# Reloading K of a half group in four transfers, one per batch, instead of one

## What is computed

```python
def attention(query, key, value):          # 8 x 128 x 512 each; key and value are both ctx
    q = (query @ Wq).reshape(nb, q_len, H, D).transpose(0, 2, 1, 3)      # H = 32, D = 128
    k = (key @ Wk).reshape(nb, q_len, KVH, D).transpose(0, 2, 1, 3)      # KVH = 8
    v = (value @ Wv).reshape(nb, q_len, KVH, D).transpose(0, 2, 1, 3)
    q = q * cos + _rotate_half(q) * sin
    k = k * cos + _rotate_half(k) * sin
    k, v = repeat(k, 4), repeat(v, 4)
    scores = where(mask == 0, -1e9, q @ k.T / sqrt(D))
    return (softmax(scores) @ v).reshape(nb, q_len, H * D) @ Wo
x = x + tanh(g_xattn) * attention(layernorm(x), ctx, ctx)
x = x + tanh(g_ffn) * (silu(x1) * x2 @ w3.T + b3)     # x1, x2 = split(layernorm(x) @ w12.T + b12)
```

## Time and profile before

| | us |
|---|---|
| median of three runs | 636.28 |
| lowest and highest | 635.9, 636.29 |
| the profiled execution, its own time | 636.77 |
| its span, first to last instruction | 634.9 |
| TensorE (PE) busy in it | 623.6 |
| POOL busy | 450.3 |
| VectorE (DVE) busy | 482.8 |
| ScalarE (ACT) busy | 319.2 |

### The profile page before, as it was taken

The page is one execution under the profiler, slowest core; times in us unless marked ns, Lnnn a source line. Parts: engine busy times, 40 slices in busy tenths (PEclk is TensorE's granted clock), DMA queues, the critical chain, the costliest instruction groups (busy, mean ns, idle before and its releaser), DMA issues.

```text
span 634.9 us, 10094 instructions
## 1 busy us (share of the span) xinstructions
PE 623.6 (98%) x2865; PEld 511.7 (81%) x2865; DVE 482.8 (76%) x1235; ACT 319.2 (50%) x893; POOL 450.3 (71%) x374
## 2 busy tenths in 40 slices
PE   8999999998999999999999999999999999999997
PEld 7888888876888877787888788888778788888886
DVE  3987675797878878788878788878885998976342
ACT  5435622554764646455455555554634657545310
POOL 6456866898889898888898898988886677601100
PEclk9999999999999999999999999999999999999999
DMA  9997995156587686776677676876645413000002
GB/s 300 324 324 227 295 321 166 70 188 211 178 266 230 201 249 207 240 244 213 196 244 241 211 245 221 261 234 213 216 139 176 131 50 90 0 2 1 0 34 99
DMA packets 133990, 118.38 MB, mean 186 GB/s; under 512 B 9776, under 2 KB 104496, under 8 KB 133936
## 3 DMA queue, kind: packets, MB, share of 16 engines
q1 hardware_dynamic: 132512, 116.69, 57.7%
q0 software_dynamic: 384, 1.05, 0.5%
q10 hardware_dynamic: 1040, 0.00, 0.1%
HBM read 72.89 MB, written 44.83 MB: 185 GB/s over the span
## 4 chain that ended last, share of the span: by engine, by line
PE 69%; DVE 9%; POOL 8%; DMA 7%; issue 4%; ACT 3%; DVEq 0%; POOLq 0%; ACTq 0%; SPq 0%
PE f_bank L889 9%; PE f_bank L891 9%; PE f_bank L890 9%; PE o_bank L889 7%; PE o_bank L891 7%; PE o_bank L890 7%; DMA p<-p_scratch 3%; DVE t_sin L2417 3%; PE pv_bank L889 3%; PE pv_bank L891 3%; PE pv_bank L890 3%; PE s_banks L889 2%; PE s_banks L891 2%; PE s_banks L890 2%; ACT prob L1492 2%
## 5 line engine op out<-in xcount | busy, mean ns | idle before, releaser
L1492 ACT ACTIVATE prob<-prob,small 128x128 f32<-128x128 f32 x256 | 99.6, 391 | 42.0 <-DVE small L2516 27.9
L889 PE MATMUL f_bank<-xT_hi,wq_hi 128*128 128x512 f32 x256 | 100.4, 392 | 0.7 <-DVE t_sin L2417 0.6
L891 PE MATMUL f_bank<-xT_hi,wq_lo 128*128 128x512 f32 x256 | 99.8, 390 | 0.0
L890 PE MATMUL f_bank<-xT_lo,wq_hi 128*128 128x512 f32 x256 | 99.8, 390 | 0.0
L889 PE MATMUL o_bank<-wo_hi,o_hi 128*128 128x512 f32 x248 | 97.9, 395 | 0.5 <-issue 0.4
L891 PE MATMUL o_bank<-wo_hi,o_lo 128*128 128x512 f32 x248 | 97.0, 391 | 0.0
L890 PE MATMUL o_bank<-wo_lo,o_hi 128*128 128x512 f32 x248 | 96.7, 390 | 0.0
L2004 POOL TENSOR_TENSOR q<-t_cos,t_sin 128x512 f32<-128x512 f32 x64 | 83.2, 1304 | 14.1 <-DVE t_sin L2417 13.7
L2417 DVE TENSOR_TENSOR t_sin<-f_bank,rope 64x512 f32<-64x512 f32 x128 | 88.1, 688 | 2.3
L1964 POOL TENSOR_TENSOR q_lo<-q,q_hi 128x512 fp32r<-128x512 f32 x64 | 82.9, 1297 | 9.5 <-ACT q_hi L1422 9.3
L2019 POOL TENSOR_TENSOR pT_lo<-p,pT_hi 128x512 fp32r<-128x512 f32 x51 | 66.2, 1297 | 22.3 <-ACT pT_hi L1422 22.3
(11 more groups left out here) (185 smaller groups left out, 1439.4 us busy)
## 6 DMA issues: line engine op xcount, KB each, us to landing
p_scratch<-p_blk SPq DMA_DIRECT2D x51, 256.0 KB, 2.1
p<-p_scratch SPq DMA_DIRECT2D x51, 256.0 KB, 3.4
s_scratch<-s_blk SPq DMA_DIRECT2D x48, 256.0 KB, 2.2
s<-s_scratch SPq DMA_DIRECT2D x48, 256.0 KB, 3.4
k_scratch<-ks_parts SPq DMA_DIRECT2D x16, 512.0 KB, 3.1
raw<-in_L_xattn_Wq_dram SPq DMA_DIRECT2D x32, 256.0 KB, 3.9
raw<-in_L_xattn_Wo_dram SPq DMA_DIRECT2D x32, 256.0 KB, 3.5
k_parts<-k_scratch SPq DMA_DIRECT2D x16, 512.0 KB, 4.6
```

Source lines behind the costliest of these rows:

```text
L889: nc.tensor.matmul(dst, st[0], mv_[0], start=start, stop=False)
L890: nc.tensor.matmul(dst, st[0], mv_[1], start=False, stop=False)
L891: return nc.tensor.matmul(dst, st[1], mv_[0], start=False, stop=stop)
L1492: e = nc.scalar.activation(prob[:, k, h, :], prob[:, k, h, :], ACT.Exp, bias=nmin[k][:, h:h + 1], scale=-1.0, accum_out=psum_row[k][:, h:h ...
```

## The change

`k_loaded` becomes four semaphores per half, one per batch. `load_k` and `next_k` take a batch b: one DMA moves that batch's 128 x 256 values (128 KB, rows of 1 KB out of the 4 KB rows of the scratch), and it waits only for the score that used this batch's old K. TensorE waits for the batch's own semaphore in front of every `scores`. Each of the 14 calls of `next_k` becomes four, mostly spread over the neighbouring exchange turns; the two loads in the first stage become eight in a row. `next_unit`, which is called nowhere, goes.

```diff
-        k_loaded = [sem(f"k_loaded{i}") for i in range(2)]
+        k_loaded = [[sem(f"k_loaded{i}{b}") for b in range(HB)] for i in range(2)]
...
-            def load_k(half, group):
-                sp.dma_start(f32(k_parts[:, half].rearrange("p b k -> p (b k)")),
-                             k_dram[bass.ds(group * 256 + half * 128, 128), :]).then_inc(k_loaded[half], 16)
+            def load_k(half, group, b):
+                sp.dma_start(f32(k_parts[:, half, b]),
+                             k_dram[bass.ds(group * 256 + half * 128, 128), b * 2 * S:(b + 1) * 2 * S]).then_inc(k_loaded[half][b], 16)
...
-                    load_k(0, 0)
-                    load_k(1, 0)
+                    for b in range(HB):
+                        load_k(0, 0, b)
+                    for b in range(HB):
+                        load_k(1, 0, b)
...
-            def next_k(half, G):
-                sp.wait_ge(pe_score, 8 * (G - 1) + 4 * half + 4)
-                load_k(half, G)
+            def next_k(half, G, b):
+                sp.wait_ge(pe_score, 8 * (G - 1) + 4 * half + b + 1)
+                load_k(half, G, b)
...
             load_chunk(0, 2)
-            next_k(0, 1)
+            next_k(0, 1, 0)
+            next_k(0, 1, 1)
             load_next_chunk(1)
...
             load_s(4)
+            next_k(0, 1, 2)
             store_p(*u(3))
             store_s(5)
             load_s(5)
+            next_k(0, 1, 3)
             load_next_chunk(3)
             load_next_chunk(4)
             load_p(*u(3))
...
+            next_k(0, 2, 0)
             store_p(*u(10))
             store_s(12)
-            next_k(0, 2)
+            next_k(0, 2, 1)
             load_s(12)
+            next_k(0, 2, 2)
             load_p(*u(10))
...
             load_s(20)
+            next_k(0, 3, 0)
             load_p(*u(18))
             store_p(*u(19))
-            next_k(0, 3)
+            next_k(0, 3, 1)
             store_s(21)
             load_next_chunk(18)
             load_p(*u(19))
             load_s(21)
+            next_k(0, 3, 2)
             store_p(*u(20))
             store_s(22)
             load_p(*u(20))
             load_next_chunk(19)
             load_s(22)
+            next_k(0, 3, 3)
...
             load_s(24)
-            next_k(1, 3)
+            next_k(1, 3, 0)
+            next_k(1, 3, 1)
             store_p(*u(23))
             store_s(25)
             load_next_chunk(22)
             load_p(*u(23))
             load_s(25)
+            next_k(1, 3, 2)
             load_next_chunk(23)
             store_p(*u(24))
             store_s(26)
             load_p(*u(24))
             load_s(26)
+            next_k(1, 3, 3)
...
             store_p(3, 2, 0)
-            next_k(0, 7)
+            next_k(0, 7, 0)
+            next_k(0, 7, 1)
+            next_k(0, 7, 2)
+            next_k(0, 7, 3)
             load_p(3, 2, 0)
             ffn_load(2)
             ffn_load(3)
             ffn_load(4)
-            next_k(1, KVH - 1)
+            next_k(1, KVH - 1, 0)
+            next_k(1, KVH - 1, 1)
+            next_k(1, KVH - 1, 2)
+            next_k(1, KVH - 1, 3)
             bias3_load()
...
                 half, b = (c // 2) % 2, 2 * (c % 2) + k
                 pe.wait_ge(act_qhi, n + 1)
                 pe.wait_ge(pool_qlo, n + 1)
-                if k == 0:
-                    pe.wait_ge(k_loaded[half], 16 * (2 * gg + c // 4 + 1))
+                pe.wait_ge(k_loaded[half][b], 16 * (2 * gg + c // 4 + 1))
```

More of the change, by code:

```diff
@@ L498, in load_chunk @@
                 sp.dma_start(dst, wq_src(G, o) if o < 4 else wo_src(G, o - 4)).then_inc(raw_loaded[o], 16)
-            def next_unit(half, G):
-                sp.wait_ge(pe_score, 8 * (G - 1) + 4 * half + 4)
-                load_k(half, G)
-                sp.wait_ge(pe_pv, 8 * (G - 1) + 4 * half + 4)
-                load_v(half, G)
             def store_p(gg, c, k):
@@ L614, in _ @@
             load_s(9)
+            next_k(1, 1, 0)
             load_next_chunk(6)
@@ L619, in _ @@
             load_p(*u(8))
-            next_k(1, 1)
+            next_k(1, 1, 1)
             load_s(10)
+            next_k(1, 1, 2)
             next_v(1, 1)
@@ L626, in _ @@
             load_s(11)
+            next_k(1, 1, 3)
+            next_k(0, 2, 0)
             store_p(*u(10))
             store_s(12)
-            next_k(0, 2)
+            next_k(0, 2, 1)
             load_s(12)
+            next_k(0, 2, 2)
             load_p(*u(10))
@@ L637, in _ @@
             load_s(13)
+            next_k(0, 2, 3)
             load_next_chunk(10)
@@ L654, in _ @@
             load_s(16)
+            next_k(1, 2, 0)
             store_p(*u(15))
-            next_k(1, 2)
+            next_k(1, 2, 1)
             store_s(17)
@@ L660, in _ @@
             load_s(17)
+            next_k(1, 2, 2)
             store_p(*u(16))
@@ L665, in _ @@
             load_s(18)
+            next_k(1, 2, 3)
             next_v(1, 2)
@@ L725, in _ @@
             load_s(29)
+            next_k(0, 4, 0)
             store_p(*u(28))
@@ L728, in _ @@
             load_next_chunk(27)
-            next_k(0, 4)
+            next_k(0, 4, 1)
             load_p(*u(28))
             load_s(30)
+            next_k(0, 4, 2)
             store_p(*u(29))
@@ L736, in _ @@
             load_s(31)
+            next_k(0, 4, 3)
             next_v(0, 4)
@@ L742, in _ @@
             load_s(32)
-            next_k(1, 4)
+            next_k(1, 4, 0)
+            next_k(1, 4, 1)
             store_p(*u(31))
@@ L748, in _ @@
             load_s(33)
+            next_k(1, 4, 2)
             store_p(*u(32))
@@ L753, in _ @@
             load_s(34)
+            next_k(1, 4, 3)
             store_p(*u(33))
@@ L763, in _ @@
             load_s(36)
+            next_k(0, 5, 0)
             load_next_chunk(33)
-            next_k(0, 5)
+            next_k(0, 5, 1)
             store_p(*u(35))
@@ L770, in _ @@
             load_s(37)
+            next_k(0, 5, 2)
             store_p(*u(36))
@@ L774, in _ @@
             load_s(38)
+            next_k(0, 5, 3)
             load_next_chunk(35)
@@ L785, in _ @@
             load_s(40)
+            next_k(1, 5, 0)
             load_next_chunk(37)
@@ L788, in _ @@
             store_s(41)
-            next_k(1, 5)
+            next_k(1, 5, 1)
             load_p(*u(39))
             load_s(41)
+            next_k(1, 5, 2)
             load_next_chunk(38)
@@ L797, in _ @@
             load_s(42)
+            next_k(1, 5, 3)
             load_next_chunk(40)
@@ L804, in _ @@
             load_s(43)
+            next_k(0, 6, 0)
             store_p(*u(42))
@@ L807, in _ @@
             load_p(*u(42))
-            next_k(0, 6)
+            next_k(0, 6, 1)
             load_s(44)
+            next_k(0, 6, 2)
             store_p(*u(43))
@@ L815, in _ @@
             load_s(45)
+            next_k(0, 6, 3)
             store_p(*u(44))
@@ L826, in _ @@
             load_s(47)
+            next_k(1, 6, 0)
             store_p(*u(46))
             store_s(48)
-            next_k(1, 6)
+            next_k(1, 6, 1)
             load_p(*u(46))
             load_s(48)
+            next_k(1, 6, 2)
             store_p(*u(47))
@@ L836, in _ @@
             load_s(49)
+            next_k(1, 6, 3)
             load_next_chunk(47)
```

## The result

The changed kernel takes 638.75 us in the median of 22 runs (636.82 to 642.56), the kernel before 637.38 beside it on the same chip: a ratio of 1.0030, 95% interval 1.0017 to 1.0043. In two later comparisons it came to 1.0017 (0.9994 to 1.0041) and 1.0036 (1.0012 to 1.0059). A ratio compares runs made beside one another, so it differs a little from that of the two medians, 1.0021 here. So the change makes this kernel slower, by 0.2 to 0.4%. Single executions scatter much more than that (the kernel before: 634 to 641 us here, and one run of 1610.51 us, far from all others), so a profile shows where time can go and the ratios say how much goes. The profiled execution of the changed kernel took 641.25 us, 2.5 above its median.

The account below looks back on a forecast made before the run. The prediction took the kernel as bound by TensorE's matmuls, busy 623.6 of 634.9 us. Its terms -0.80, -0.30 and +0.3 summed to -0.8 us, giving 635.5 us against the median of 636.28, range 633.8 to 637.5.

Parts of the forecast that it names:

- the count of SP time: 48 more DMA issues on SP at 0.44 us, 21 us, nearly all beside other work; costed at nothing.
- -0.80 at 294.52: K issued at 280.74, two of four pieces leave: TensorE's 0.73 us gap goes, plus 0.07; bounds 0 and -0.80.
- -0.30 at 266.27: K issued at 256.03, one of four pieces stays: the 0.23 us gap before the output projection goes, plus 0.07.
- The 0.07 us: First matmul after a TensorE gap takes 0.47 us against 0.40; counted as gained when the gap goes.
- The turn at 486.54: Unit 52, all four pieces between store and load of p: load issued 0.09 us later, rows 0.2; +0.3 us.
- the first load at 78 us: Two K issues become eight in the first stage; what stands behind up to 2.6 us later, taken as 0.
- The three unpaused loads of p: Units 3, 10 and 18: a piece straight ahead delays each load 0.44 us; taken as nothing, at most 1.3 us.
- B: Rival, faster by more: all idle time from 200 to 500 us goes, gain 2.6 us, 633.7; chance 0.27.
- D: Rival, nothing moves: the two gaps reappear later because POOL sets the pace, 0 to +0.3, 636.4 us; chance 0.20.
- C: Rival, slower: four issues at 486.54 cost more than 0.44 us each, load of p late, 638.0 us; chance 0.18.
- wrong altogether: Signs refuting the whole forecast: a TensorE wait naming k_parts, or a gap from 50 to 114 us.
- right: Signs: gaps at 266 and 294 gone, unit 23's store near 3 us, unit 19's load under 4.5, pieces 2 to 4.

Follow-up runs that it names:

- the halves: Kernel before with K in two transfers of two batches: both at the old place 1.0015; the second behind the next load of scores 0.9999.
- spread halves: Kernel before with K in two transfers of two batches, the second moved behind the next load of scores: 0.9999 (0.9986 to 1.0012).

## Why the prediction was wrong

- **The step that failed** is the count of SP time: "that is 21 us of SP's time, nearly all beside other work: most of the new pieces stand right behind the load of scores, where SP next waits for DVE", costed at 0. Four transfers for one cost 3.5 us with nothing moved (1.0055; 1.0063 with long rows), and K whole behind a load of scores, the place called free, came to 1.0066. The step counted what the pieces take of SP and left out what they do to the exchange transfer that comes next on the queue. In the change SP's pauses inside the turns did not grow (21.0 us before, 21.4, 21.5 and 23.4 after); the landings of the stores did in two of its three profiles (250.3 before and 241.5 with the waits alone; 266.4, 256.3 and 251.5 after). The pause of SP behind a load of scores was read from one execution as slack; in the changed kernel's chain of waits that place carries the piece and everything behind it. The rule of the Trainium skill that I cited, "DMA: Bandwidth & Descriptors", section "Rules for kernel authors", to join small transfers, had the sign. My reply, that a fixed part costs only him who waits, overlooked who waits: not an engine for K, but the exchange behind K.
- **The forecast gains were priced from one execution.** -0.80 at 294.52: that gap is gone in all three profiles of the change. But in the kernels that leave K whole at its place it is 0.20 us (the waits alone), 0.15 (small transfers behind K) and nothing (short rows), so most of the 0.73 belonged to that one execution. -0.30 at 266.27: the turn of unit 19 shortened by 0.5 us, yet the gap is 1.00, 0.39 and nothing in the three profiles, not clearly less than with K whole (0.23 before, and 0.44, 0.07 and nothing in those three kernels). The 0.07 us by which a matmul behind a gap was taken to be longer does not come back with the gap: the one at 298.98 has none ahead of it and takes 0.47. The reasoning on the turns from which K was taken was right in direction; it was not set against the turns into which the pieces went.
- **The turn at 486.54** (+0.3): the load of p goes 0.22 us after its store has landed (store at 490.04, 2.33 us; load at 492.59), near the 0.1 forecast, and takes 4.69 us against 4.43. The gap at its pv is 0.73, and 0.31 and nothing in the later profiles; moving the pieces behind the load brought nothing (1.0045). The gap of 0.25 at 499.95, to which the prediction led this turn's chain, is not K's: it is 0.26 us also where K stands behind that load (pieces, whole load, or four whole loads moved).
- **The sum:** 636.77 less 0.8 is 635.97, not 635.95; nothing hangs on it.
- **Costs taken as 0 that can't be told from 0:** TensorE's waits (1.0003), the first load at 78 us (64.00 of 64). The rows of 1 KB, 0.2 at one place, came to 1.0013 over all reloads, not to be told from 1. The three unpaused loads of p: not the loss.
- **The rivals.** B fell. D's reappearing idle time was there, but POOL, less busy than before, did not set it. C had the sign and nearly the time (638.0; the ratio gives 1.003 x 636.28 = 638.2), by luck, since the mechanism was another than its own: four issues at 486 us took 1.77 us in all, and the loss lies in the loop.
- **What "wrong altogether" named**, a wait for k_parts or a gap before 114 us, did not happen. Most of what "right" named did happen: the store of p of unit 23 took 2.23 us, the load of unit 19 3.27, the pieces of K 3.3 in the median. All these signs look at places that K left or at K itself. I had none for a longer exchange turn where the pieces went, the thing that moved.

**What stays open.** That one large transfer, issued first, moves its bytes while SP issues the rest, and that four in a row, or a late one, push theirs into the exchange behind, fits the pair of small transfers ahead and behind, both ways of four pieces and the halves. It is argued from them and from the sums of one execution each; no run measured the sharing itself. That longer turns make the kernel longer is argued too: the two go together. It does not say why one piece behind each store is so much dearer than the same piece behind each load of scores; the stores land later alike in both (276.9 and 278.6 us), the loads in the first alone (354.4 against 346.0). Which reload of the change gives and which takes is read from single executions only. And no version was shown faster than the kernel before: the two best, four reloads moved whole (636.11 against 636.68) and spread halves (636.41 against 636.68), have intervals that hold 1.

## What to carry to other kernels

Where one queue issues all transfers of a store-and-load loop, a transfer's price is what it does to the loop's transfers behind it, even if nobody ever waits for the transfer itself: count each issue (about 0.45 us here) and its bytes against the next turn, at every place it is put. A pause in the issuing queue's list in one execution is no slack, and a gap in one execution is no price: look at several profiles, and test a place by putting one harmless transfer there, ahead of and behind the suspected one. Nothing tried here was shown to beat the large reload left whole and issued ahead of the small things around it.

## What the runs showed of the hardware

The order of the same transfers on one queue can matter where their number does not: 48 transfers of 64 bytes, 0.9997 behind K and 1.0074 ahead of it. Issues on SP scatter: a piece of K took 0.32 us at best, 0.50 in the median and 1.32 at worst in the changed kernel's first profile, and 2.12 at worst in its second (0.44 and 0.78 for the whole loads before). Loads that are issued later behind a large transfer can land sooner by as much: with the small transfers behind K the pauses ahead of the loads grew from 21.0 to 34.0 us in sum, and the landings of the loads fell from 349.3 to 337.6. The landing of an unchanged transfer differs between executions: the load of K took 4.6 us in the median in the kernel before and 4.2 in the one with TensorE's waits alone, so its 3.7 and 3.6 with small transfers behind and ahead of it are no effect of their order.
